# A 5x5 correlation layer on one core: pixels stored in natural order, and Gram products that read their moving columns eight apart

## The chip, the cores and the metric

The kernel runs on one core of one Trainium2 chip. The metric is the device time of one execution in microseconds, lower is better. Engines are named as in the profile: PE is TensorE (PEld its weight loads), DVE is VectorE, ACT is ScalarE, POOL is GpSimd, SP the engine that only issues DMAs.

## What is computed

The input is x, 16 images of 512 channels and 64 x 64 pixels, float32. The first layer normalises in groups and correlates every pixel with its 5 x 5 neighbours over all channels; the 25 numbers, scaled to length one, join the 512 channels as input of a 1 x 1 convolution. The second layer pools each channel plane with one of several window sizes. The change touches the first layer only.

```python
def spatial_descriptor(x, k):
    xp = jnp.pad(x, ((0, 0), (0, 0), (p, p), (p, p)))
    corrs = [jnp.sum(x * jax.lax.dynamic_slice(xp, (0, 0, di, dj), (b, c, h, w)), axis=1)
             for di in range(k) for dj in range(k)]
    return jnp.stack(corrs, axis=1)
gs = spatial_descriptor(x, 5)                       # x = group norm of the input
gs = gs / jnp.sqrt(jnp.sum(gs * gs, axis=1, keepdims=True) + 1e-6)
out = relu(einsum('bchw,oc->bohw', concatenate([x, gs], axis=1), W) + bias)
x = x + out                                         # first layer
x = x + pooled_mix(_gn(x), w1, b1, w2, b2)          # second layer
```

## The kernel before

**Tiling.** Channels lie on the 128 partitions, in four groups (`CT`). An image is worked through in 8 chunks (`CH`) of 8 rows, that is 512 pixels. A chunk is four pairs of rows, `u`, of 128 pixels each. In a pair the pixel in row `r` and column `w = 8j + k` has the natural place 64r + 8j + k; `k` is its column class. `turned` is a view over a natural chunk that runs through it class by class (u, k, r, j), so that neighbours in it lie eight places apart; `classed` is the plain view of a chunk that is stored in that order.

**What the engines do with a chunk.** ACT normalises each channel group twice, into a float32 copy `g32` and a float16 copy `gh` (lines 506 and 508). It reads x through `turned` and writes class by class. DVE subtracts the two and gives the low part `gl` (713). So each float32 value becomes two float16 values, and each product needs three matmuls. `gh` and `gl` are rings of four chunks.

On PE a Gram product (`gram`, line 1056 through `product`) takes a pair of rows as stationary operand (128 pixels) and that pair and the next as moving operand (256 columns): 12 matmuls into a bank of PSUM, all pixel products of the two pairs. DVE multiplies the block by a mask of column distances into `bq` (`mask`, 726, 731, 732). The block of pair and next pair is also needed the other way round: PE transposes it (`turn_blocks`, 1114), ACT copies it to `bq` (`after`, 528). `picks` (1101) gathers the correlations of one row distance and column class from the blocks by matmuls with 0/1 matrices `pick`, each onto 32 partitions; four of them stand side by side, one for two classes. Then come the norm (535, 1123, 537, 745, 749), a split into float16 on POOL (409, 411) and 12 small DMAs that regroup it into `tpair` (`regroup` on SP).

The convolution over the 512 channels (`conv`, 1079 to 1081) is 48 matmuls of 512 columns a chunk; `tail` (1134) adds the 25 correlations by 8 matmuls of 256 columns, one chunk later. ACT takes the sum out of PSUM with bias and relu (`conv_out`, 520), class by class in and by `turned` out, DVE adds x and takes statistics (738, 740).

**Order.** Every engine has its order written by hand, the same for every image. On PE a chunk is: picks, first Gram product of the next chunk, norm, second Gram product, tail of the chunk before, third and fourth Gram product, a quarter of the convolution, the transposes, the rest of the convolution. At `c == STATS_AT` (4) the two small matmuls for the next image's group norm stand between (1142, 1146). Before the first Gram product PE waits for `s_gl`: the low parts of the chunk after next. Each engine waits on semaphores that the others count up. ACT may be two `g32` buffers ahead of DVE. Beyond the first layer only line 853 matters here, a DVE operation in the preparation of the second: it reads one of the four adjacent values of each of 64 records (`recs`), so 64 float32 values 16 bytes apart; line 816 there has the same form with adjacent values. Line 599 is an activation of the second layer, PSUM to SBUF without a stride.

The stages of the second layer follow when the last chunk is stored.

Of the kernel before, what the change touches and what calls it, by code (L numbers as in the profile page):

```python
# [16 lines left out]
C, H, W = 512, 64, 64  # L17
# [4 lines left out]
CW = ROWS * W  # L22
NB = H // 2
PAIRS = ROWS // 2
PRING = 2 * PAIRS
AFTER, SAME, BEFORE = range(3)
KS = 5
# [7 lines left out]
RING = 4  # L35
# [5 lines left out]
REP = 3 * 32  # L41
QUADS = 4
# [3 lines left out]
def const_arrays():  # L46


    p = np.arange(P)
    k, r, j = p // 16, p // 8 % 2, p % 8  # L50
    w = 8 * j + k
    band = (np.abs(w[:, None] - w[None, :]) <= KS // 2).astype(np.float32)


    pick = np.zeros((P, 3, 2, QUADS, 32), np.float32)
    for role in range(3):
        for e in range(2):
            for t in range(QUADS):
                di = r + 2 * (1 - role) - e
                rho = (k - 2 * t + 2) % 8  # L60
                ok = (np.abs(di) <= KS // 2) & (rho < 6)
                pick[p[ok], role, e, t, (rho * KS + di + 2)[ok]] = 1.0
    ssum = (p[:, None] // 32 == p[None, :] // 32).astype(np.float32) * 2.0 ** -12
    gavg = (p[:, None] // CG == p[None, :] // CG).astype(np.float32) / CG
    ident = np.eye(P, dtype=np.float32)
    before = (p[:, None] < p[None, :]).astype(np.float32)
    ones = np.ones((P, P), np.float32)
    return np.concatenate([band, pick.reshape(P, -1), ssum, gavg, ident, before, ones], axis=1)
# [18 lines left out]
def build(nc, x, wt, wturn, bias, w1t, b1, w2t, b2, consts, out):  # L87
    fp32, fp16, i32 = mybir.dt.float32, mybir.dt.float16, mybir.dt.int32
    ALU, ACT, AX = mybir.AluOpType, mybir.ActivationFunctionType, mybir.AxisListType
# [17 lines left out]
    with ctx:  # L107
# [3 lines left out]
        def sb(name, shape, dt):  # L111
            return ctx.enter_context(nc.sbuf_tensor(name, shape, dt))
# [3 lines left out]
        o = 0  # L116
        band = cst[:, o:o + P]; o += P
# [7 lines left out]
        bias_sb = sb("bias_sb", [P, CT], fp32)  # L125
# [10 lines left out]
        gbias = sb("gbias", [P, CT], fp32)  # L136
# [7 lines left out]
        def take(n):  # L144
            pos[0] += n
            assert pos[0] <= ARENA
            return arena[:, pos[0] - n:pos[0]]

        take(2 * CT * PIX)
        gh = take(CT * RING * CW // 2).bitcast(fp16).rearrange("p (t n) -> p t n", t=CT)  # L150
        gl = take(CT * RING * CW // 2).bitcast(fp16).rearrange("p (t n) -> p t n", t=CT)
        g32 = take(2 * CW).rearrange("p (s n) -> p s n", s=2)
# [7 lines left out]
        tpair = take(CW).bitcast(fp16).rearrange("p (s n) -> p s n", s=2)  # L160
        relu = take(2 * CW).rearrange("p (s n) -> p s n", s=2)
# [64 lines left out]
        psum = ctx.enter_context(nc.psum_tensor("psum", [P, 8, 512], fp32))  # L226
# [70 lines left out]
        def xs(ct, lo, n, par):  # L297

            return arena[:, bass.ds(par * (CT * PIX) + (ct * PIX + lo), n)]

        def turned(a):

            return a.rearrange("p (u r j k) -> p u k r j", r=2, j=8, k=8)

        def classed(a):

            return a.rearrange("p (u k r j) -> p u k r j", k=8, r=2, j=8)

        def gram_parts(t):


            parts, row = [], 2 * t
            while row < min(2 * t + 4, H):
                end = min(2 * t + 4, H, (row // (RING * ROWS) + 1) * RING * ROWS)
                parts.append(((row - 2 * t) * W, (row % (RING * ROWS)) * W, (end - row) * W))
                row = end
            return parts
# [170 lines left out]
        def _(act):  # L488
# [5 lines left out]
            def normalise(i, c, first=False, between=None):  # L494

                n0 = (i * CH + c) * CT
                act.wait_ge(s_newton, 3 * i + 3)
                if not first:

                    act.wait_ge(s_chunk_used, i * CH + c - RING + 1)  # L500
                for ct in range(CT):
                    if not (isinstance(n0, int) and n0 + ct < 2):
                        act.wait_ge(s_gl, n0 + ct - 1)
                    act.sem_inc(s_carry_a, 1)
                    piece = turned(xs(ct, c * CW, CW, i % 2))
                    act.activation(classed(g32[:, ct % 2, :]), piece, ACT.Identity, bias=gbias[:, ct:ct + 1],  # L506
                                   scale=grstd[:, ct:ct + 1])
                    act.activation(classed(gh[:, ct, (c % RING) * CW:(c % RING + 1) * CW]), piece, ACT.Identity,  # L508
                                   bias=gbias[:, ct:ct + 1], scale=grstd[:, ct:ct + 1]).then_inc(s_gh, 1)
                    if between and ct == 1:  # L510
                        between()

            def conv_out(chunk, o):
                n = chunk * CT + o
                act.wait_ge(s_conv, n + 1)
                if isinstance(n, int) and n < 2:
                    pass
                else:
                    act.wait_ge(s_added, n - 1)
                act.activation(turned(relu[:, o % 2, :]), classed(psum[:, o, :]), ACT.Relu, bias=bias_sb[:, o:o + 1],  # L520
                               scale=1.0 / (SC * SC)).then_inc(s_relu, 1)

            def after(i, c):
# [34 lines left out]
            for c in range(3):  # L558
                normalise(0, c, first=True)
# [6 lines left out]
            for o in range(CT):  # L566
                conv_out(B * CH - 1, o)
# [486 lines left out]
        def _(pe):  # L1054
            def product(dst, w, m, k, nk):
                return pe.matmul(dst, w, m, start=(k == 0), stop=(k == nk - 1))  # L1056

            def gram(i, t):
                if not (isinstance(i, int) and i == 0 and t < 2):
                    pe.wait_ge(s_masked, i * NB + t - 1)  # L1060
                own = ((2 * t) % (RING * ROWS)) * W
                for col, ring, n in gram_parts(t):
                    for ct in range(CT):
                        sh, sl = gh[:, ct, own:own + 2 * W], gl[:, ct, own:own + 2 * W]
                        mh, ml = gh[:, ct, ring:ring + n], gl[:, ct, ring:ring + n]
                        dst = psum[:, GRAM0 + t % 2, col:col + n]
                        product(dst, sh, mh, 3 * ct, 3 * CT)
                        product(dst, sh, ml, 3 * ct + 1, 3 * CT)
                        last = product(dst, sl, mh, 3 * ct + 2, 3 * CT)
                last.then_inc(s_gram, 1)  # L1070
# [14 lines left out]
            def picks(i, c):  # L1085

                pe.wait_ge(s_after, i * CH + c + 1)
                if not (isinstance(i, int) and i == 0 and c == 0):
                    pe.wait_ge(s_fn, i * CH + c)
                half = (c % 2) * PAIRS * P  # L1090
                for e in range(2):
                    for k, role in enumerate((BEFORE, AFTER, SAME)):

                        u0 = 1 if role == BEFORE and c == 0 else 0
                        u1 = PAIRS - 1 if role == AFTER and c == CH - 1 else PAIRS
                        src = bq[:, role, half:half + PAIRS * P]\
                            .rearrange("p (u t q r j) -> p t r q u j", t=QUADS, q=2, r=2, j=8)
                        for t in range(QUADS):
                            dst = psum[32 * t:32 * t + 32, BANK_A, 0:QW]\
                                .rearrange("p (q u r j) -> p r q u j", q=2, r=2, j=8)  # L1100
                            last = pe.matmul(dst[:, e, :, u0:u1, :], pick[:, role, e, t, :], src[:, t, e, :, u0:u1, :],
                                             start=(e == 0 and k == 0), stop=True, skip_group_check=True)
                last.then_inc(s_pick, 1)
# [21 lines left out]
            def tail(i, c):  # L1125


                half = c % 2
                pe.wait_ge(grouped[half], (i * (CH // 2) + c // 2 + 1) * GROUPED)
                src = tpair[0:REP, half, :].rearrange("p (t q u s) -> p q u t s", t=QUADS, q=2, u=PAIRS)  # L1130
                for o in range(CT):
                    dst = psum[:, o, :].rearrange("p (u t q s) -> p q u t s", u=PAIRS, t=QUADS, q=2)
                    for par in range(2):
                        last = pe.matmul(dst[:, par], wd[0:REP, par * C + o * P:par * C + (o + 1) * P],  # L1134
                                         src[:, par], start=False, stop=True, skip_group_check=True)
                    last.then_inc(s_conv, 1)
# [49 lines left out]
            if B > 2:  # L1186
                with pe.Fori(1, B - 1) as i:
                    image(i, False)
            image(B - 1, True)
            tail(B - 1, CH - 1)  # L1190


# [92 lines left out]
```

## Time and profile before

| | us |
|---|---|
| median of 3 runs (4600.07 to 4608.84) | 4606.43 |
| profiled execution, its time | 4614.89 |
| profiled execution, its span | 4613.1 |
| mean granted TensorE clock of the span | 0.928 |

The span begins with the first instruction and ends with the last; 1.8 us of the execution's time lie around it. Each busy time is a sum over a group of instructions; matmuls overlap in the pipeline, so the time from one matmul's start to the next one's start, and not the duration of one, says how fast they go. A share of busy time is a mean over two layers that have different limits, so it has to be read by stretch.

### The profile page before, as it was taken

What the parts mean: (1) busy time and instruction counts of PE and PEld (TensorE: products, weight loads), DVE (VectorE), ACT (ScalarE), POOL (GpSimd) and SP (SyncE); (2) the same over time, 40 slices, a digit from 0 to 9 for tenths busy, and PEclk for the clock granted to TensorE, in tenths of its full rate; (3) what the DMA queues carried; (4) which work ended last, traced back from release to release, by engine and by line L of the source; (5) the groups of instructions that cost most, each with busy time, mean ns of one, the idle gap of its engine ahead of it and who ended that gap; (6) DMA issues with size and microseconds to landing.
All of it is one profiled execution on the core that took longest, in us unless ns stands there. A gap on an engine that the chain in (4) does not pass through costs nothing. (4 is left out here: it accounts for less than half of the span.)

```text
span 4613.1 us, 73329 instructions
## 1 busy us (share of the span) xinstructions
PE 3847.0 (83%) x23656; PEld 2135.8 (46%) x23657; DVE 3520.3 (76%) x4010; ACT 2589.7 (56%) x2830; POOL 637.1 (14%) x624
## 2 busy tenths in 40 slices
PE   3999999999999999999989767898888777777665
PEld 2655555555555555555556443343333333323222
DVE  5676667667666765766665576899999999999994
ACT  4777777777777777777777434443333233232322
POOL 0000000000000000000000012333232322222221
PEclk9999999999999999999999878898899888888887
DMA  4233322323333232333321246553333333323221
GB/s 167 97 116 116 109 103 100 134 98 116 116 116 111 99 120 97 116 116 116 115 98 61 61 129 217 180 182 154 146 147 134 132 143 125 134 107 123 111 119 48
DMA packets 174313, 556.98 MB, mean 121 GB/s; under 512 B 91248, under 2 KB 91248, under 8 KB 157552
## 3 DMA queue, kind: packets, MB, share of 16 engines
q1 hardware_dynamic: 152016, 283.62, 17.7%
q0 software_dynamic: 21920, 268.59, 15.1%
q8 instruction: 206, 3.38, 0.3%
q14 instruction: 171, 1.40, 0.1%
HBM read 277.23 MB, written 274.86 MB: 120 GB/s over the span
## 5 line engine op out<-in xcount | busy, mean ns | idle before, releaser
L931 DVE TENSOR_TENSOR arena<-arena 128x2048 f32<-128x2048 f32 (+4 forms) x730 | 1759.1, 2430 | 107.7 <-ACT arena L579 66.3
L1250 PE MATMUL psum<-arena 128*128 128x512 f32 x1072 | 615.0, 658 | 442.0 <-issue 399.0
L1056 PE MATMUL psum<-arena 128*128 128x256 f16 (+1 forms) x6344 | 744.2, 272 | 152.7 <-DVE arena L713 134.8
L579 ACT ACTIVATE arena<-arena 128x4096 f32<-128x4096 f32 x67 | 244.2, 3645 | 972.3 <-DVE arena L931 706.6
L1079 PE MATMUL psum<-arena 128*128 128x512 f16 x2048 | 782.3, 382 | 0.7 <-ACT arena L520 0.7
L1080 PE MATMUL psum<-arena 128*128 128x512 f16 x2048 | 782.3, 382 | 0.0
L1081 PE MATMUL psum<-arena 128*128 128x512 f16 x2048 | 782.1, 382 | 0.0
L520 ACT ACTIVATE arena<-psum,bias_sb 128x512 f32<-128x512 f32 x512 | 577.5, 1184 | 270.6 <-PE psum L1134 171.3
L1056 PEld LDWEIGHTS psum<-arena 128*128 128x128 f16 x6344 | 597.4, 99 | 241.5 <-issue 124.1
L713 DVE TENSOR_TENSOR arena<-arena 128x512 f16<-128x512 f32 x512 | 351.7, 687 | 432.0 <-ACT arena L508 431.9
L506 ACT ACTIVATE arena<-arena,gbias,grstd 128x512 f32 (+1 forms) x512 | 669.3, 1307 | 6.0 <-DVE arena L713 4.7
L508 ACT ACTIVATE arena<-arena,gbias,grstd 128x512 f16 (+1 forms) x512 | 668.6, 1306 | 0.0
L1254 PE MATMUL psum<-arena 128*128 128x512 f32 x1072 | 579.9, 624 | 0.0
L1250 PEld LDWEIGHTS psum<-arena 128*128 128x128 f32 x1072 | 217.7, 210 | 738.3 <-issue 674.3
L599 ACT ACTIVATE arena<-psum,arena 128x512 f32<-128x512 f32 x536 | 336.0, 689 | 321.8 <-PE psum L1254 321.4
L1252 PE MATMUL psum<-arena 128*128 128x512 f32 x896 | 500.7, 642 | 0.0
L738 DVE TENSOR_TENSOR arena<-arena 128x512 f32 (+1 forms) x512 | 349.4, 682 | 141.8 <-ACT arena L520 141.8
L740 DVE BATCH_NORM_STATS2 bny<-arena 128x6 f32 (+1 forms) x512 | 355.4, 694 | 98.2 <-DVE arena L738 96.0
L409 POOL CAST arena<-arena 128x128 f16<-128x128 f32 x128 | 37.4, 292 | 2510.4 <-DVE arena L749 2510.4
L1254 PEld LDWEIGHTS psum<-arena 128*128 128x128 f32 x1072 | 219.2, 204 | 290.1 <-issue 290.1
L663 DVE BATCH_NORM_STATS2 bnx<-arena 128x6 f32 (+1 forms) x512 | 326.2, 681 | 11.3 <-DMA arena<-in_x 11.2
L1081 PEld LDWEIGHTS psum<-arena 128*128 128x128 f16 x2048 | 201.6, 98 | 245.5 <-issue 7.0
(138 smaller groups left out, 2672.0 us busy)
## 6 DMA issues: line engine op xcount, KB each, us to landing
arena<-in_x SPq DMA_DIRECT2D x64, 2048.0 KB, 12.6
y_planes<-arena SPq DMA_DIRECT2D x64, 2048.0 KB, 7.9
arena<-arena SPq DMA_DIRECT2D x1536, 8.0 KB, 1.7
arena<-plane_records,arena POOLq DMA_INDIRECT x67, 3.0
arena<-y_planes,arena POOLq DMA_INDIRECT x67, 9.4
out<-arena POOLq DMA_INDIRECT x67, 8.7
arena<-in_wt SPq DMA_DIRECT2D x1, 1024.0 KB, 12.6
cst<-in_consts SPq DMA_DIRECT2D x1, 768.0 KB, 4.3
```

The costliest lines, as they stand in the source:

```text
L506: act.activation(classed(g32[:, ct % 2, :]), piece, ACT.Identity, bias=gbias[:, ct:ct + 1], scale=grstd[:, ct:ct + 1])
L508: act.activation(classed(gh[:, ct, (c % RING) * CW:(c % RING + 1) * CW]), piece, ACT.Identity, bias=gbias[:, ct:ct + 1], scale=grstd[:, ct ...
L520: act.activation(turned(relu[:, o % 2, :]), classed(psum[:, o, :]), ACT.Relu, bias=bias_sb[:, o:o + 1], scale=1.0 / (SC * SC)).then_inc(s_ ...
L740: dve.bn_stats(bny[:, o, c, :], y).then_inc(s_y, 1)
L931: ins = dve.tensor_tensor(dst, a, b, ALU.max)
L1056: return pe.matmul(dst, w, m, start=(k == 0), stop=(k == nk - 1))
L1079: pe.matmul(dst, h, gh[:, ct, slot], start=(ct == 0), stop=False)
L1080: pe.matmul(dst, h, gl[:, ct, slot], start=False, stop=False)
L1081: last = pe.matmul(dst, l, gh[:, ct, slot], start=False, stop=(ct == CT - 1))
L1250: pe.matmul(dst, diag[:, s, 0, :], bufs[:, u, b * CW:(b + 1) * CW], start=True, stop=False)
L1252: pe.matmul(dst, diag[:, s, 1, :], small[:, s, b * ROWS:(b + 1) * ROWS, 1:W + 1], start=False, stop=False)
L1254: pe.matmul(dst, diag[:, s, 2, :], big[:, s, b * CW:(b + 1) * CW], start=False, stop=True)\
```

## The change

No instruction is added, removed or moved on any engine; the operands' access patterns and two constant tables change.

- ACT reads x and writes `g32` and `gh` in natural order (506, 508), and takes the convolution's result out of PSUM in natural order (520). `turned` and its strides are gone from ACT.
- The Gram products read the moving operand `gh` or `gl` with consecutive columns eight float16 values apart (16 bytes), through a view that now bears the name `classed`. The stationary operand is read in natural order. A block therefore has natural pixels on its partitions and classes along its columns.
- The mask and the `pick` matrices follow. The transposed block has natural pixels along its columns, so `picks` reads the blocks of role AFTER with columns eight float32 values apart (32 bytes).
- `tail` writes to PSUM with columns two float32 apart (8 bytes), and its moving operand runs through the four quarters `t` first, 128 float16 values apart.

```diff
     p = np.arange(P)
-    k, r, j = p // 16, p // 8 % 2, p % 8
-    w = 8 * j + k
-    band = (np.abs(w[:, None] - w[None, :]) <= KS // 2).astype(np.float32)
+    w_col = 8 * (p % 8) + p // 16
+    band = (np.abs(p[:, None] % W - w_col[None, :]) <= KS // 2).astype(np.float32)
...
     for role in range(3):
+        r, k = (p // 8 % 2, p // 16) if role == AFTER else (p // W, p % 8)
...
-        def turned(a):
+        def classed(a):
 
             return a.rearrange("p (u r j k) -> p u k r j", r=2, j=8, k=8)
-
-        def classed(a):
-
-            return a.rearrange("p (u k r j) -> p u k r j", k=8, r=2, j=8)
...
-                    piece = turned(xs(ct, c * CW, CW, i % 2))
-                    act.activation(classed(g32[:, ct % 2, :]), piece, ACT.Identity, bias=gbias[:, ct:ct + 1],
+                    piece = xs(ct, c * CW, CW, i % 2)
+                    act.activation(g32[:, ct % 2, :], piece, ACT.Identity, bias=gbias[:, ct:ct + 1],
                                    scale=grstd[:, ct:ct + 1])
-                    act.activation(classed(gh[:, ct, (c % RING) * CW:(c % RING + 1) * CW]), piece, ACT.Identity,
+                    act.activation(gh[:, ct, (c % RING) * CW:(c % RING + 1) * CW], piece, ACT.Identity,
                                    bias=gbias[:, ct:ct + 1], scale=grstd[:, ct:ct + 1]).then_inc(s_gh, 1)
...
-                act.activation(turned(relu[:, o % 2, :]), classed(psum[:, o, :]), ACT.Relu, bias=bias_sb[:, o:o + 1],
+                act.activation(relu[:, o % 2, :], psum[:, o, :], ACT.Relu, bias=bias_sb[:, o:o + 1],
                                scale=1.0 / (SC * SC)).then_inc(s_relu, 1)
...
-                        mh, ml = gh[:, ct, ring:ring + n], gl[:, ct, ring:ring + n]
+                        mh, ml = classed(gh[:, ct, ring:ring + n]), classed(gl[:, ct, ring:ring + n])
...
-                            .rearrange("p (u t q r j) -> p t r q u j", t=QUADS, q=2, r=2, j=8)
+                            .rearrange("p (u r j t q) -> p t r q u j" if role == AFTER else
+                                       "p (u t q r j) -> p t r q u j", t=QUADS, q=2, r=2, j=8)
...
-                src = tpair[0:REP, half, :].rearrange("p (t q u s) -> p q u t s", t=QUADS, q=2, u=PAIRS)
+                src = tpair[0:REP, half, :].rearrange("p (t q s) -> p q s t", t=QUADS, q=2)
                 for o in range(CT):
-                    dst = psum[:, o, :].rearrange("p (u t q s) -> p q u t s", u=PAIRS, t=QUADS, q=2)
+                    dst = psum[:, o, :].rearrange("p (s t q) -> p q s t", t=QUADS, q=2)
```

## Rows read from the trace of the kernel before

**Rows 1.** The profile's page: slices of the span, busy tenths of PE, DVE and ACT
```profile
PE   3999999999999999999989767898888777777665
...
DVE  5676667667666765766665576899999999999994
ACT  4777777777777777777777434443333233232322
```
**Rows 2.** Busy time by stretch: from, to, length, then each engine; first layer, second
```profile
100.00:2560.00 2460.00, 2269.44 (x19712) 1426.38 (x19711) 1635.74 (x3022) 1862.42 (x1864) 89.19 (x248) 0.99 0.30 107
...
2580.00:4613.00 2033.00, 1529.50 (x3523) 677.59 (x3520) 1823.62 (x879) 669.05 (x912) 546.22 (x367) 0.86 0.36 134
```
**Rows 3.** Waits of PE, 100 to 2560: total us, times, longest
```profile
PE psum L1056 <- DVE arena L713: 120.6, 80, 1.9
PE psum L1101 <- issue: 33.4, 15, 3.0
PE psum L1142 <- ACT arena L528: 26.4, 15, 1.8
```
**Rows 4.** Waits of DVE in the same stretch
```profile
DVE arena L713 <- ACT arena L508: 402.5, 299, 2.2
```
**Rows 5.** Timeline of PE from c = 1 on: start, us, then what; starts of picks
```profile
1213.72 0.88 PE L1101 MATMUL psum<-arena,cst 128*32 128x64 f32 x48
1216.51 1.48 PE L1056 MATMUL psum<-arena 128*128 128x256 f16 x12 [1.92 <-DVE arena L713]
...
1272.89 0.88 PE L1101 MATMUL psum<-arena,cst 128*32 128x64 f32 x48
...
1374.39 0.88 PE L1101 MATMUL psum<-arena,cst 128*32 128x64 f32 x48
```
**Rows 6.** The same view, the chunk c = 5, and the next one's start
```profile
1296.84 0.88 PE L1101 MATMUL psum<-arena,cst 128*32 128x64 f32 x48
1297.65 1.48 PE L1056 MATMUL psum<-arena 128*128 128x256 f16 x12
...
1300.50 1.04 PE L1134 MATMUL psum<-arena 96*128 96x256 f16 x8
1301.38 2.79 PE L1056 MATMUL psum<-arena 128*128 128x256 f16 x24
1304.00 0.38 PE L1079 MATMUL psum<-arena 128*128 128x512 f16 x1
...
1314.89 0.88 PE L1101 MATMUL psum<-arena,cst 128*32 128x64 f32 x48
```
**Rows 7.** Groups by line and form, whole span: busy us, mean ns, idle before
```profile
L506 ACT ACTIVATE arena<-arena,gbias,grstd 128x512 f32 x448 | 585.9, 1308 | 4.7 <-DVE arena L713 4.7
L520 ACT ACTIVATE arena<-psum,bias_sb 128x512 f32<-128x512 f32 x512 | 577.5, 1184 | 270.6 <-PE psum L1134 171.3 <-DVE arena L738 87.9 <-issue 0.2
...
L713 DVE TENSOR_TENSOR arena<-arena 128x512 f16<-128x512 f32 x512 | 351.7, 687 | 432.0 <-ACT arena L508 431.9
...
L599 ACT ACTIVATE arena<-psum,arena 128x512 f32<-128x512 f32 x536 | 336.0, 689 | 321.8 <-PE psum L1254 321.4
```
**Rows 8.** Groups of PE by form, 0 to 2700: the Gram products and the tail
```profile
L1056 PE MATMUL psum<-arena 128*128 128x256 f16 x5760 | 711.4, 277 | 150.2 <-DVE arena L713 134.8 <-DVE arena L726 15.4
...
L1134 PE MATMUL psum<-arena 96*128 96x256 f16 x1024 | 133.0, 272 | 0.0
...
L1056 PE MATMUL psum<-arena 128*128 128x128 f16 x576 | 37.4, 219 | 0.0
```
**Rows 9.** Groups of DVE by form, 2631 to 2644: 64 elements, 16 bytes apart or adjacent
```profile
L853 DVE TENSOR_TENSOR arena<-arena 128x64 f32<-128x64 f32 x1 | 0.3, 269 | 0.0
...
L816 DVE TENSOR_TENSOR arena<-arena 128x64 f32<-128x64 f32 x1 | 0.2, 226 | 0.0
```
**Rows 10.** Timeline at the start: first and last normalising activation of three chunks
```profile
45.21 1.30 ACT L506 ACTIVATE arena<-arena,gbias,grstd 128x512 f32<-128x512 f32 x1 [1.33 <-DVE gbias L703]
...
72.73 1.28 ACT L508 ACTIVATE arena<-arena,gbias,grstd 128x512 f16<-128x512 f32 x1
```

## The prediction, made before the changed kernel ran

> **What bounds the kernel now.** I read the page's slices first [rows 1]: two layers, with the border a little after the middle. PE is at nine tenths in the first, DVE in the second. The table by stretch says the same in sums [rows 2]: from 100 to 2560 us PE is busy 2269 of 2460 us at a clock of 0.99, ACT 1862, DVE 1636. The change touches only the first layer, so the second keeps its time, and the question is what it does to PE's time in the first.
>
> Next the waits of PE [rows 3]. Nearly all of them come from ACT in the end: 120.6 us for the low parts, which DVE makes as soon as ACT has written the copies (DVE itself waits 402.5 us for that [rows 4]), 26.4 us for the copy at line 528, and 33.4 us before the picks at c = 0, where the names end at "issue" and the picks of role AFTER wait for the same copy. The timeline shows it chunk by chunk: 1.92 us before the first Gram product [rows 5], none at c = 5 [rows 6]. The chunk c = 5, with no wait, takes 1314.89 - 1296.84 = 18.05 us; a whole image takes 1374.39 - 1213.72 = 160.67 us [rows 5, 6]. Eight chunks of 18.05 are 144.4, and about 0.2 less because some Gram products and picks are shorter. So **16.5 us an image, 264 us in 16 images**, are waits and what follows from them (c = 4 alone, from 1272.89 to 1296.84, is 23.95 us). That is the most that a faster ACT can give back. The rest is PE's own work.
>
> **The change part by part.**
>
> *ACT gets lighter.* The normalising activation takes 1308 ns with a stride of eight float32 on its input, and the relu 1184 ns with that stride on its output; the nearest one of 512 elements without a stride takes 689 ns [rows 7]. A chunk has 8 of the first and 4 of the second: 8 x 0.62 + 4 x 0.50 = 6.9 us less of ACT's time, from about 15 of 20 us to 8. With that ACT is no longer what anyone waits for, and I give back all of the 264 us but 30: some latency stays (picks to square to norm, the group statistics), and DVE with 15 to 16 us a chunk is then close behind. So -234.
>
> *The start.* Three chunks are normalised before PE gets going: 24 activations from 45.21 on, 27.52 / 23 = 1.20 us from one to the next, and the third Gram product can't start before their low parts are through [rows 10]. At some 0.6 us each this is 24 x 0.6 = 14 us less. At the end the last four relus give 2 us. So -16.
>
> *The Gram products' moving operand.* This decides. How many columns: 5760 matmuls of 256 and 576 of 128 are 1.548 million columns [rows 8]. Their present pace is (1304.00 - 1301.38) / 24 = 109 ns for 256, that is 0.426 ns a column [rows 6]. No row of PE with a stride of this kind exists, so I bound it. Below: 0, if the stride costs nothing; a gain in these matmuls themselves is excluded, since they keep their columns and their order. Above, rows of other engines: ACT takes (1308 - 689) / 512 = 1.2 ns an element more for its stride of 32 bytes, up to 1.20 us / 512 = 2.3 ns an element in all [rows 7, 10]; DVE with 16 bytes between elements (line 853) takes 269 against 226 ns for 64 [rows 9], 0.67 ns an element more than its (687 - 226) / 448 = 1.03 ns for adjacent ones [rows 7, 9], so 1.70 in all. So neither engine reads separated places at its own full pace, and DVE's is the nearest row, having the same 16 bytes. Two readings of it are possible for PE. As a ratio (DVE 1.65 times, ACT 2 to 2.5 times) it says about twice. As an absolute time for each separate place (1.70 ns) it says about four times. For the ratio speaks that PE's reading is wider than one stream needs: the picks take four different streams from the same partitions side by side, 48 matmuls of 64 float32 columns in 1297.65 - 1296.84 = 0.81 us [rows 6], which is 256 bytes in 17 ns, or 16 bytes each 1.05 ns over the four. **I take twice**, 0.85 ns a column, and keep four times as a rival. At twice: 1.548 million x 0.426 = +660 us.
>
> *The tail.* 1024 matmuls of 256 columns [rows 8], 0.88 us for 8 [rows 6], so again 0.43 ns a column. Both its ends lose their runs: the input jumps 256 bytes from column to column, the output goes 8 bytes apart. I take the same factor as for the Gram products: 128 chunks x 0.88 = +113 us. Bounds: 0, and three times that.
>
> *The picks.* Of 48 matmuls 16 read float32 columns 32 bytes apart. In each of the four streams a column takes 4 x 17 / 64 = 1.05 ns already, which is more than the 0.85 assumed above, so I take 0. At twice their pace they would cost 16 x 17 ns x 128 = +35 us, kept for the range.
>
> *Masks, transposes, DVE, POOL, DMA.* Same shapes, all contiguous or with the runs they had: 0. DVE's 16 us a chunk lie beside PE's 18, and more safely beside the 24 that come out.
>
> **The sum** on the profiled execution: 4614.9 - 234 - 16 + 660 + 113 = 5138. That execution lies 8.5 us above the median, so 5130 as a median. A chunk would take 18.05 + 48 x 0.109 + 0.88 = 24.2 us.
>
> **A rule weighed.** Rows 9 show that elements 16 bytes apart are not free for DVE. The Trainium skill, SBUF — State Buffer, section Door 1: The DMA port swizzle, says that SBUF has lines of 16 bytes, that two accesses to a line are needed for full pace, and in the same note that a stride of up to eight 16-bit elements is free. By the first half, one column a line is a penalty of a size that it doesn't give, and the sum stays as it is; by the second, eight float16 values are still free and the time is the 4356 of the free-stride rival below. The same note says that PSUM has lines of 8 bytes and that any access with gaps slows matmuls much; that speaks against the tail, and no row here shows it.
>
> **The rivals.**
>
> *The stride is free; the result is faster.* If PE's reading works ahead well enough, the Gram products keep 109 ns. Then 4614.9 - 234 - 16 - 8.5 = 4356; with the tail alone at twice its time 4470. For it: PE reads runs of 16 float16 in the tail and of 8 float32 in the picks without a visible price, and it sustains four streams. Against it: both engines that show a stride in this trace pay for it. The turning point is where the price eats the 250 us: 250 / (1.548 + 0.262 million columns) = 0.14 ns a column, so 0.56 ns against 0.426, 1.3 times.
>
> *Each separate place costs a fixed time, as on DVE and ACT.* At four times, 1.70 ns a column: 3 x (660 + 113) - 250 + 4606 = 6675. That is DVE's 1.70 ns as well. At the 2.3 ns of ACT it would be 1.81 million x 1.87 - 250 + 4606 = 7740. For it: the two engines have different clocks and still both land near 2 ns. Against it: the four streams of the picks.
>
> *ACT's gain is not a gain.* If PE's waits came from DVE itself, the 234 us would stay: 5370 at twice. Against it: DVE waits 402.5 us for ACT [rows 4].
>
> **How the numbers follow.** Twice the time for a column: 0.43, with 4980 (tail free, all waits gone) to 5370 (waits stay, picks dearer); single value 5130. Four times, DVE's rate: 0.29, 6400 to 6850. Between these two, near three times: 0.04. ACT's rate or worse: 0.06, 7000 to 7800. Free or nearly free: 0.18, 4340 to 4580, of which 0.01 is too near to tell. So the range goes from 4950 to 6850: 0.76 in full, and a little of the edges. The likeliest case's own range is 4980 to 5370. A measurement of this kernel tells about 0.2% from no change: faster 0.17, within 0.2% 0.01, slower 0.82.
>
> **What would show each step.** In the profile of the changed kernel: line 506 and 520 near 0.65 to 0.69 us; 12 Gram matmuls spaced 0.22 us (0.11 if free, 0.43 if a fixed price); the tail 1.8 us for 8; 16 picks of each 48 at their old pace; a chunk of 24.2 us at every c, with no wait left for line 713, and ACT idle more than half the time. The second layer keeps its length. The prediction is wrong if the spacing of the Gram matmuls is not about twice, since each tenth of their pace is worth 66 us; everything else together moves 150 us at most.

## The result: 1.53 times the time, above the range

The changed kernel takes 7054.09 us (median of 4 runs, 7050.44 to 7057.37) against 4603.25 us for the kernel before: a ratio of 1.5324, with a 95% interval from 1.5298 to 1.5351. The direction was forecast, the size was not: the single value was 5130 us, and the range ended at 6850 us. The profiled execution of the changed kernel has a span of 7052.6 us, so it is 2439.5 us longer than the one of before.

The line numbers are a little lower in the changed file: the Gram products stand at line 1053, the convolution at 1076 to 1078, the picks at 1099, the tail at 1132, the activations at 503, 505 and 517. The first view is the page's slices, as in [rows 1], with the granted clock. The first layer now fills 29 of 40 slices, ACT is busy for about a quarter of it, and the clock is low in it:

```profile
PE   7999999999999999999999999999868888776775
...
ACT  2222222222222222222222222222134433333232
...
PEclk8766666666666666676766666666689998888887
```

The timeline of PE shows one chunk (start in us, duration of the merged row, then what); it answers to [rows 6]:

```profile
2503.88 1.13 PE L1099 MATMUL psum<-arena,cst 128*32 128x64 f32 x48
2504.94 5.58 PE L1053 MATMUL psum<-arena 128*128 128x256 f16 x12
2510.34 0.60 PE L1121 MATMUL psum<-arena,cst 128*128 128x128 f32 x2
2510.74 5.60 PE L1053 MATMUL psum<-arena 128*128 128x256 f16 x12
2516.16 3.66 PE L1132 MATMUL psum<-arena 96*128 96x256 f16 x8
2519.64 8.32 PE L1053 MATMUL psum<-arena 128*128 128x256 f16 x24
2527.78 0.61 PE L1076 MATMUL psum<-arena 128*128 128x512 f16 x1
2528.18 0.63 PE L1077 MATMUL psum<-arena 128*128 128x512 f16 x1
...
2541.08 1.01 PE L1099 MATMUL psum<-arena,cst 128*32 128x64 f32 x48
```

Twelve Gram matmuls take 2510.34 - 2504.94 = 5.40 us, where they took 1.32: 0.450 us each, 1.76 ns a column, **4.1 times**. The row with 24 Gram matmuls takes less than twice that (8.14 us), since it holds 12 of 256 columns and 12 of only 128, for the last pair of rows of an image. The tail takes 2519.64 - 2516.16 = 3.48 us for 8, where it took 0.88. And something is there that the prediction doesn't have: the first convolution matmuls behind the Gram products start 0.40 to 0.43 us apart, twice the usual 0.216. The table by stretch of that same chunk (from, to, length, busy times, then the granted clock, the third number from the end) says why:

```profile
2505.00:2507.00 2.00, 2.00 (x7) 0.52 (x6) 0.00 (x0) 0.28 (x1) 0.00 (x0) 1.00 0.03 8
2507.00:2510.00 3.00, 3.00 (x8) 0.83 (x7) 0.00 (x0) 0.00 (x0) 0.00 (x0) 0.83 0.00 0
2510.00:2513.00 3.00, 3.00 (x9) 1.18 (x8) 1.67 (x3) 0.37 (x1) 0.00 (x0) 0.50 0.00 0
2528.00:2532.00 4.00, 4.00 (x10) 1.36 (x9) 3.41 (x6) 1.97 (x3) 0.00 (x0) 0.50 0.00 0
2534.00:2541.00 7.00, 7.00 (x34) 3.04 (x31) 1.39 (x2) 2.71 (x4) 0.00 (x0) 1.00 1.01 354
```

PE is busy in all of them. The granted clock is at its upper level (2.4 GHz) when the Gram products begin, falls to its lower one (1.2 GHz) inside the first of them, and it is up again only inside the convolution. The first Gram product, most of it at the upper level, and the second, at the lower one, go at the same pace, 5.40 and 5.42 us for 12. So their time doesn't come from the clock; the clock's fall comes with them, and matmuls with adjacent columns pay for it.

ACT's side came out as intended. The groups by line, in the place of [rows 7]:

```profile
L517 ACT ACTIVATE arena<-psum,bias_sb 128x512 f32<-128x512 f32 x512 | 351.9, 687 | 1656.8 <-DVE arena L735 865.3 <-PE psum L1132 791.5
...
L503 ACT ACTIVATE arena<-arena,gbias,grstd 128x512 f32 (+1 forms) x512 | 411.0, 803 | 20.8 <-DVE arena L710 19.4 <-DVE gbias L700 1.3
```

The relu fell from 1184 to 687 ns, the normalising activation from 1308 to 803 ns (0.69 was forecast). Of PE's waits [rows 3] one is left between 100 and 5000 us, the one before the picks at c = 0:

```profile
PE psum L1099 <- issue: 28.6, 14, 2.5
```

### The profile page after: what moved, and what is told of

It is laid out like the page before. It is cut to its first block and busy times, and to the rows that moved or that the text cites. A ratio compares the mean times of both kernels' runs of the same rounds, so it can differ in the third digit from the quotient of the medians.

```text
span 7052.6 us, 73329 instructions
## 1 busy us (share of the span) xinstructions
PE 6472.4 (92%) x23656; PEld 2470.1 (35%) x23657; DVE 3566.1 (51%) x4010; ACT 1888.7 (27%) x2830; POOL 643.8 (9%) x624
## 5 line engine op out<-in xcount | busy, mean ns | idle before, releaser
L1053 PE MATMUL psum<-arena 128*128 128x256 f16 (+1 forms) x6344 | 2799.1, 609 | 12.7 <-DVE arena L710 9.5
L723 DVE TENSOR_TENSOR arena<-psum,cst 128x256 f32<-128x256 f32 x448 | 190.3, 425 | 2455.9 <-PE psum L1053 2455.9
L1053 PEld LDWEIGHTS psum<-arena 128*128 128x128 f16 x6344 | 775.7, 124 | 1819.1 <-issue 1732.6
L1076 PE MATMUL psum<-arena 128*128 128x512 f16 x2048 | 872.6, 426 | 0.0
L1077 PE MATMUL psum<-arena 128*128 128x512 f16 x2048 | 871.0, 425 | 0.0
L1078 PE MATMUL psum<-arena 128*128 128x512 f16 x2048 | 857.2, 419 | 0.0
L517 ACT ACTIVATE arena<-psum,bias_sb 128x512 f32<-128x512 f32 x512 | 351.9, 687 | 1656.8 <-DVE arena L735 865.3
L1248 PEld LDWEIGHTS psum<-arena 128*128 128x128 f32 x1072 | 217.0, 209 | 737.9 <-issue 654.9
L1132 PE MATMUL psum<-arena 96*128 96x256 f16 x1024 | 468.2, 614 | 0.0
L503 ACT ACTIVATE arena<-arena,gbias,grstd 128x512 f32 (+1 forms) x512 | 411.0, 803 | 20.8 <-DVE arena L710 19.4
L505 ACT ACTIVATE arena<-arena,gbias,grstd 128x512 f16 (+1 forms) x512 | 410.1, 801 | 0.0
```

What stands on the lines that cost most here:

```text
L503: act.activation(g32[:, ct % 2, :], piece, ACT.Identity, bias=gbias[:, ct:ct + 1], scale=grstd[:, ct:ct + 1])
L505: act.activation(gh[:, ct, (c % RING) * CW:(c % RING + 1) * CW], piece, ACT.Identity, bias=gbias[:, ct:ct + 1], scale=grstd[:, ct:ct + 1]) ...
L1076: pe.matmul(dst, h, gh[:, ct, slot], start=(ct == 0), stop=False)
L1077: pe.matmul(dst, h, gl[:, ct, slot], start=False, stop=False)
L1078: last = pe.matmul(dst, l, gh[:, ct, slot], start=False, stop=(ct == CT - 1))
L1248: pe.matmul(dst, diag[:, s, 0, :], bufs[:, u, b * CW:(b + 1) * CW], start=True, stop=False)
```

## The experiments

**Theory A**: the time comes from PE's reading of separated places in SBUF, a fixed time for each, whatever its clock. **Theory B**: it is mostly the clock. **Theory C**: the tail pays for its separated writes to PSUM. The first four runs take the parts apart. Each kernel ran once, beside one run of the kernel before, which gave 4618.49 us for these four. The seven runs of the kernel before in a later group lie between 4590.54 and 4616.65 us, so a difference of some 20 us between two single runs says nothing.

*The changed kernel with plain Gram reads.*

```diff
-                        mh, ml = classed(gh[:, ct, ring:ring + n]), classed(gl[:, ct, ring:ring + n])
+                        mh, ml = gh[:, ct, ring:ring + n], gl[:, ct, ring:ring + n]
```

> The changed kernel with one thing undone: the Gram products read their moving columns side by side again (the values in the blocks then stand in natural order, so the output isn't the reference's; as many instructions of the same shapes). Theory A, each separate 16-byte place read costs PE about 1.76 ns a column whatever its clock: the Gram products go back to 0.11 us each, the clock stays up in the convolution behind them, the tail stays at 0.435 us a matmul and costs 128 x 2.6 = 333 us, the picks 32 us, ACT's lighter work gives 250 back: 4606 + 333 + 32 - 250 = 4721 us. Theory B, most of the loss is the falling clock and what hangs on it and the tail's writes set that off too: the clock stays near 0.7 in the first layer and the time stays above 5500 us.

Measured: 4765.08 us. One chunk in its timeline of PE:

```profile
1300.56 1.13 PE L1099 MATMUL psum<-arena,cst 128*32 128x64 f32 x48
1301.62 1.49 PE L1053 MATMUL psum<-arena 128*128 128x256 f16 x12
1302.94 0.39 PE L1121 MATMUL psum<-arena,cst 128*128 128x128 f32 x2
...
1304.47 3.65 PE L1132 MATMUL psum<-arena 96*128 96x256 f16 x8
1307.94 2.83 PE L1053 MATMUL psum<-arena 128*128 128x256 f16 x36
```

The Gram products are back at 1302.94 - 1301.62 = 1.32 us for 12 (the row of 36 holds 24 of only 128 columns), the tail still takes 3.47 us, the picks 1.06 instead of 0.81 us. The clock is 0.99 from 100 to 2500 us. With this one edit 2290 of the 2450 us are gone, and the low clock with them, so the total alone doesn't part theory A from B. The paces do: the Gram matmuls of the changed kernel kept theirs when the clock fell, and the tail takes 3.47 us here (1217.81 to 1221.28 in another chunk) at the upper level, as at the lower one in the changed kernel:

```profile
1217.90:1221.20 3.30, 3.30 (x9) 0.83 (x8) 1.72 (x5) 1.81 (x3) 0.72 (x2) 1.00 0.03 5
```

Theory B falls with that. The stride in picks and tail costs 0.25 + 2.59 us a chunk, 364 us in 128; the time is 147 us above that of before, so the lighter ACT gave back 217 us, and theory A's 4721 us was 44 too low.

*The same, and the tail reads runs.*

```diff
-                src = tpair[0:REP, half, :].rearrange("p (t q s) -> p q s t", t=QUADS, q=2)
+                src = tpair[0:REP, half, :].rearrange("p (t q s) -> p q t s", t=QUADS, q=2)
...
-                    dst = psum[:, o, :].rearrange("p (s t q) -> p q s t", t=QUADS, q=2)
+                    dst = psum[:, o, :].rearrange("p (s t q) -> p q t s", t=QUADS, q=2)
```

> As the run with plain Gram reads, and the tail runs through its columns in another order: it reads 64 adjacent float16 values at a time and writes them to PSUM 32 bytes apart (same result of the tail as in the changed kernel). Theory A, the price is one of reading SBUF: the tail goes back to 0.11 us a matmul and the time to 4606 - 250 + 32 = 4388 us. Theory C, it is the separated writes to PSUM that cost in the tail: its matmuls stay at 0.435 us or get slower, and the time is 4721 us or more.

Measured: 4541.14 us, between the two expectations, and the timeline says why:

```profile
1222.41 1.89 PE L1132 MATMUL psum<-arena 96*128 96x256 f16 x8
1224.09 1.08 PE L1053 MATMUL psum<-arena 128*128 128x256 f16 x8
```

8 matmuls in 1.68 us, 0.21 us each: neither the 0.11 of adjacent columns nor the 0.435 of the changed kernel. A separated write to PSUM costs too, twice the pace of adjacent ones, 0.82 ns a column; a separated read costs four times. Theories A and C were half right on the tail.

*The kernel before with the Gram stride alone.*

```diff
-                        mh, ml = gh[:, ct, ring:ring + n], gl[:, ct, ring:ring + n]
+                        mh, ml = (a[:, ct, ring:ring + n].rearrange("p (a k) -> p k a", k=8) for a in (gh, gl))
```

> The kernel before with one thing of the change alone: the Gram products read their moving columns eight float16 values apart (the values in the blocks stand in another order, so the output isn't the reference's). ACT, picks and tail are those of before. Theory A: 1.548 million columns x 1.336 ns = +2068 us, clock loss in the first quarter of the convolution 128 x 2.5 = +320, the waits of PE for ACT vanish behind it, -250: 6745 us. If the strides of tail and picks carried a large part of the loss instead, this run would be well under 6400 us.

Measured: 6839.94 us, of the changed kernel's loss the largest part by far. Its timeline shows the price and the clock's part beside it:

```profile
1208.75 5.58 PE L1056 MATMUL psum<-arena 128*128 128x256 f16 x12
1214.15 0.61 PE L1123 MATMUL psum<-arena,cst 128*128 128x128 f32 x2
...
1219.98 1.89 PE L1134 MATMUL psum<-arena 96*128 96x256 f16 x8
1221.66 8.33 PE L1056 MATMUL psum<-arena 128*128 128x256 f16 x24
```

The Gram products take 5.40 us for 12 again. The tail, which in this kernel reads and writes runs of 16, takes 1.68 us for 8 where it took 0.88: it runs behind the Gram products at the lower level. That is up to 128 x 0.80 = 102 us, which the expectation doesn't have; it is 95 us below the measured time. Its other terms are off too and cancel in part: summed from start to start over the trace, the convolution takes 232 us more than before and not 320, and PE's idle time shrinks by 168 us and not 250.

*Natural order everywhere.* This kernel computes what the reference does; the picks pay instead of the Gram products.

```diff
-    band = (np.abs(p[:, None] % W - w_col[None, :]) <= KS // 2).astype(np.float32)
+    band = (np.abs(p[:, None] % W - p[None, :] % W) <= KS // 2).astype(np.float32)
...
-        r, k = (p // 8 % 2, p // 16) if role == AFTER else (p // W, p % 8)
+        r, k = p // W, p % 8
...
-                            .rearrange("p (u r j t q) -> p t r q u j" if role == AFTER else
-                                       "p (u t q r j) -> p t r q u j", t=QUADS, q=2, r=2, j=8)
+                            .rearrange("p (u r j t q) -> p t r q u j", t=QUADS, q=2, r=2, j=8)
```

with plain Gram reads and the tail of the second run.

> A kernel with natural order everywhere: Gram products read side by side, mask and pick matrices follow, all 48 picks of a chunk read float32 columns 32 bytes apart, the tail reads runs and writes to PSUM 32 bytes apart. Theory A (reads cost, PSUM writes don't): picks cost 16 ns more for each of 48, 0.77 us a chunk, 98 us in all, ACT's 250 us come back: 4606 + 98 - 250 = 4454 us, faster than both kernels. Theory C (writes cost): 333 us or more on top, 4790 us, slower than before.

Measured: 4590.39 us. The picks take 1.54 us for 48 as expected; the time is 136 us above theory A's 4454: 104 us are the tail's writes, and some 30 us of ACT's 250 didn't come back. In each of the four streams a pick now takes 4 x 1540 / 48 / 64 = 2.0 ns for a float32 value at a place of its own; why that is more than the 1.76 ns of the Gram products isn't tested here.

```profile
1257.19 1.60 PE L1097 MATMUL psum<-arena,cst 128*32 128x64 f32 x48
1258.73 1.48 PE L1052 MATMUL psum<-arena 128*128 128x256 f16 x12
```

**What exactly is paid for?** Theory D: each visit to a 16-byte place costs some 1.76 ns, however many columns it serves. Theory E: each column that isn't adjacent to the last does. F: only strides from 16 bytes on cost. G: the price grows with the distance. Three runs are the kernel before with another number in the place of `k=8` in the diff above (2, 4 and 16 columns' distance); the fourth is a kernel built on theory D. The runs of before beside these have a median of 4608.54 us.

> The kernel before, its Gram products read their moving columns two float16 values apart, 4 bytes, in two runs (values in the blocks in another order, so the output isn't the reference's). Theory D: four columns share a 16-byte place, so 0.44 ns a column, as now: 0.11 to 0.115 us a matmul, 4610 to 4650 us. Theory E: 0.45 us a matmul, as with 16 bytes, 6840 us.

Measured: 4603.23 us.

```profile
1214.71 1.53 PE L1056 MATMUL psum<-arena 128*128 128x256 f16 x12 [1.82 <-DVE arena L713]
1216.09 0.38 PE L1123 MATMUL psum<-arena,cst 128*128 128x128 f32 x2
```

> As before with the Gram products' moving columns four float16 values apart, 8 bytes (output isn't the reference's). Theory D: two columns share a 16-byte place, 0.88 ns a column, 0.225 us a matmul; 1.548 million x 0.46 = +712, PE's waits vanish behind it, -230: 5090 us. Theory E: 6840 us. Theory F, only a stride of 16 bytes or more costs: 4610 us.

Measured: 5128.14 us.

```profile
1232.49 2.88 PE L1056 MATMUL psum<-arena 128*128 128x256 f16 x12
1235.19 0.40 PE L1123 MATMUL psum<-arena,cst 128*128 128x128 f32 x2
```

> As before with the Gram products' moving columns sixteen float16 values apart, 32 bytes (output isn't the reference's). Theory D: still one place a column, 0.45 us a matmul, 6840 us as with 16 bytes. Theory G, the price grows with the distance, as line 506 on ACT with 32 bytes is dearer for an element than DVE with 16: 2.1 to 2.3 ns a column, 0.54 to 0.59 us a matmul, 7400 us or more.

Measured: 6847.71 us.

```profile
1210.07 5.69 PE L1056 MATMUL psum<-arena 128*128 128x256 f16 x12
1215.58 0.61 PE L1123 MATMUL psum<-arena,cst 128*128 128x128 f32 x2
```

Start to start, for 12 matmuls of 256 columns:

| distance of columns | us for 12 | ns a column | columns in 16 bytes | ns for 16 bytes |
|---|---|---|---|---|
| 2 bytes (before) | 1.32 | 0.43 | 8 | 3.44 |
| 4 bytes | 1.38 | 0.45 | 4 | 1.80 |
| 8 bytes | 2.70 | 0.88 | 2 | 1.76 |
| 16 bytes | 5.40 | 1.76 | 1 | 1.76 |
| 32 bytes | 5.51 | 1.79 | 1 | 1.79 |

Theory D holds from 8 bytes on: a place costs 1.76 to 1.79 ns. At 2 bytes the columns' own pace of 0.43 ns is the longer of the two, and at 4 bytes the two nearly coincide (4 x 0.43 = 1.72 ns). E falls with the rows of 4 and 8 bytes, F with that of 8, G with that of 32, which is 2% dearer than 16. The tail's reads in the changed kernel, 256 bytes apart, take 435 / 256 = 1.70 ns. At 8 bytes the clock stays up (0.99 from 100 to 2500 us), at 16 and 32 bytes it doesn't (0.69).

*A kernel built on it.* The picks take the two classes of a quarter innermost, so each visit serves two float32 values, and they write their columns in runs of 16 (not all 64 side by side, as the expectation has it). The tail's reads are then 4 bytes apart, which costs nothing; its writes stay 32 bytes apart. Against the kernel with natural order everywhere (the indices of `dst` and `src` in the matmul follow):

```diff
-                            .rearrange("p (u r j t q) -> p t r q u j", t=QUADS, q=2, r=2, j=8)
+                            .rearrange("p (u r j t q) -> p t r u j q", t=QUADS, q=2, r=2, j=8)
...
-                                .rearrange("p (q u r j) -> p r q u j", q=2, r=2, j=8)
+                                .rearrange("p (u r j q) -> p r u j q", q=2, r=2, j=8)
...
-                src = tpair[0:REP, half, :].rearrange("p (t q s) -> p q t s", t=QUADS, q=2)
+                src = tpair[0:REP, half, :].rearrange("p (t s q) -> p q t s", t=QUADS, q=2)
```

> The kernel with natural order everywhere, and the picks run through the two classes of a quarter innermost: each reads two adjacent float32 values (8 bytes) and then jumps 32 bytes, and writes its 64 columns to PSUM side by side; the tail's moving operand is then read with columns two float16 apart (4 bytes), its writes stay 32 bytes apart. Theory D, reading costs about 1.76 ns for each visit to a 16-byte place, whatever is taken from it up to its contents: a pick pays 0.9 ns a column, below the 1.05 ns that it takes anyway, and the picks go back from 1.53 to 0.8 us a chunk: 4590 - 128 x 0.72 = 4498 us, faster than before by 2.4%. Theory E, every column that isn't adjacent to the last costs 1.76 ns: half of the picks' columns still pay, and the tail's reads at 4 bytes cost as in the changed kernel: about 4590 - 50 + 224 = 4760 us.

Measured: 4511.05 us, 0.9797 times the kernel before (0.9767 to 0.9826). It is faster than both kernels of this case.

```profile
1221.19 0.91 PE L1097 MATMUL psum<-arena,cst 128*32 128x64 f32 x48
1222.04 1.48 PE L1052 MATMUL psum<-arena 128*128 128x256 f16 x12
...
1224.89 1.89 PE L1130 MATMUL psum<-arena 96*128 96x256 f16 x8
1226.58 2.82 PE L1052 MATMUL psum<-arena 128*128 128x256 f16 x24
```

The expectation by theory D was 4498 us; E's 4760 is out. The picks are back at 0.85 us for 48. The tail's 1.69 us for 8 is what its writes cost; 104 us of ACT's gift are still lost there.

**The tail's two ends, one at a time, and the clock.** The kernel before took 4609.55 us beside these three. The first two are the changed kernel with plain Gram reads, and one end of the tail made contiguous:

```diff
-                src = tpair[0:REP, half, :].rearrange("p (t q s) -> p q s t", t=QUADS, q=2)
+                src = tpair[0:REP, half, :].rearrange("p (q s t) -> p q s t", t=QUADS, q=2)
```

> The run with plain Gram reads, and the tail reads its moving columns side by side but writes as in the changed kernel, 8 bytes apart (the tail's values land in wrong places, so the output isn't the reference's). If a separated write to PSUM costs the same at 8 as at 32 bytes, the tail takes 0.211 us a matmul, as in the run whose tail reads runs: 4541 us. If 8 bytes are free or dearer, it shows: 0.11 us and 4437 us, or above 0.25 us.

Measured: 4544.07 us; 8 tail matmuls in 1241.59 - 1239.90 = 1.69 us:

```profile
1239.90 1.89 PE L1132 MATMUL psum<-arena 96*128 96x256 f16 x8
1241.59 0.64 PE L1053 MATMUL psum<-arena 128*128 128x256 f16 x4
```

```diff
-                    dst = psum[:, o, :].rearrange("p (s t q) -> p q s t", t=QUADS, q=2)
+                    dst = psum[:, o, :].rearrange("p (q s t) -> p q s t", t=QUADS, q=2)
```

> The run with plain Gram reads, and the tail writes its columns side by side but reads as in the changed kernel, each column 256 bytes from the last (output isn't the reference's). If the 0.435 us of the tail's matmuls in the changed kernel are the reads alone, and the slower writes hide behind them, it stays at 0.435 us and the time at 4765 us. If reads and writes add up, it falls to about 0.33 us, 4660 us.

Measured: 4802.56 us; 8 tail matmuls in 3.46 us:

```profile
1257.25 3.64 PE L1132 MATMUL psum<-arena 96*128 96x256 f16 x8
1260.71 4.12 PE L1053 MATMUL psum<-arena 128*128 128x256 f16 x24
```

So writes 8 and 32 bytes apart cost the same 0.21 us a matmul, reads 256 bytes apart 0.43, and the larger price hides the smaller. The 37 us above the run with plain Gram reads show in the second row: the 24 Gram matmuls behind this tail took 4.12 us and not 2.80, at a granted clock of 0.69 from 1261 to 1265 us. In this run the clock fell behind some of the tails. Summed from start to start over the trace, the Gram matmuls of the first layer take 42 us more than in that run.

*One Gram product of four.*

```diff
-                        mh, ml = gh[:, ct, ring:ring + n], gl[:, ct, ring:ring + n]
+                        mh, ml = (a[:, ct, ring:ring + n].rearrange("p (a k) -> p k a", k=8 if t % 4 == 0 else 1) for a in (gh, gl))
```

> The kernel before with the 16-byte stride in one Gram product of four, the first of each chunk, 12 matmuls of 48 (values in those blocks in another order, so the output isn't the reference's). The price for a read is the same, 0.45 us a matmul: +128 x 12 x 0.342 = +525 us. If the clock stays up since the stretch is short, nothing is added, and PE's waits shrink by some 200: 4930 us. If the clock falls in each chunk as it does with all four, the matmuls behind it are slower too, up to 214 us in all: 5140 us.

Measured: 5290.57 us, above both expectations. Three timeline rows, two stretches of the same chunk, then PE's and ACT's waits from 100 to 2500 us:

```profile
1240.79 5.58 PE L1056 MATMUL psum<-arena 128*128 128x256 f16 x12
...
1246.59 2.77 PE L1056 MATMUL psum<-arena 128*128 128x256 f16 x12
1249.15 1.18 PE L1134 MATMUL psum<-arena 96*128 96x256 f16 x8
```

```profile
1241.00:1243.00 2.00, 2.00 (x5) 0.47 (x4) 0.69 (x1) 0.61 (x2) 0.00 (x0) 1.00 0.04 8
1246.80:1248.80 2.00, 2.00 (x11) 1.45 (x10) 1.27 (x3) 0.37 (x1) 0.00 (x0) 0.50 0.00 0
```

```profile
PE psum L1056 <- DVE arena L713: 79.8, 60, 1.9
```

```profile
ACT arena L537 <- PE psum L1123: 593.8, 95, 6.8
```

In the kernel before, from 100 to 2560 us, that last row is:

```profile
ACT arena L537 <- PE psum L1123: 257.9, 124, 2.8
```

The price is the forecast one, 5.40 us for 12, +525 us. With this one product the clock falls in 124 of 127 chunks, and the second Gram product, with adjacent columns, takes 1249.15 - 1246.59 = 2.56 us instead of 1.31. Summed from start to start over the trace, this makes the Gram products 127 us dearer beyond the 525, the tail 42 and the norm's matmuls 20. And PE's waits stay: 79.8 us for the low parts in 95 chunks, against 120.6 in 124 before [rows 3]. I had thought that a slower PE gives ACT time. It doesn't here. ACT itself waits for the norm (line 1123), which stands behind that first Gram product: 593.8 us in 95 waits, 6.3 us a chunk, where it was 2.1. What is put before the norm lengthens ACT's chunk as well as PE's. 525 + 127 + 42 + 20 = 714 us stand against the 681 measured; PE's idle time is 20 us less than before and the convolution's time 15.

## Why the prediction was wrong

**The bound was right.** PE set the first layer before and sets it now, as forecast; the second layer kept its length (1978 us from its first group statistics at 5075.0 to the end, 1982 us from 2631.2 before).

**The step that failed: twice instead of four times.** The bounds for a column with a 16-byte stride were right, 0.426 to 2.3 ns, and DVE's row [rows 9] gave 1.70 ns a place, which is within 4% of the 1.76 that PE takes. (It is an estimate from single instructions of 64 elements, so that it comes so near may be luck.) I had this number and used it as a ratio of engine paces. The picks that spoke for it [rows 6] have four streams side by side, each with 1.05 ns a column and four columns to a place: 4.2 ns a place for a stream. They are slower than 1.76 ns a place and so say nothing on what one stream can do; I had divided by the four streams. The other support, ACT's "2 to 2.5 times", was too high as well: against its own activations without a stride in the changed kernel, 1308 to 803 ns and 1184 to 687 ns, it is 1.6 to 1.7 times, and the stride's price is 1.0 ns an element and not 1.2. With 1.76 ns the Gram products' term is 1.548 million x 1.336 = 2068 us, not 660.

**The term that was missing: the clock.** No part of the prediction asked what a slower stream does to the granted clock. The 6144 convolution matmuls have 254 us more of duration than before (872.6 + 871.0 + 857.2 against 782.3 + 782.3 + 782.1); at the lower level a duration grows by 0.25 us (0.38 to 0.63) and the distance of two starts by 0.21, so this is 254 x 0.21 / 0.25 = 213 us of time. Without it the time would be some 6841 us, just inside the range. The rival "each separate place costs a fixed time" is the one that came true in its mechanism; it was worked out at 6675 us, with a Gram price of 3 x 660 = 1980 and no clock. That 7054 lies between the 7000 and 7800 us given to "ACT's rate or worse" is chance: the price of a place was near DVE's rate.

**The tail and the picks.** The tail's term was 113 us by the same factor and is 128 x 2.60 = 333 us. Its separated writes alone would be 104 us. With the reads at four times, 3 x 113 = 339 us, the term comes out too. The picks were taken at nothing; the 16 with the stride cost 0.25 us a chunk, 32 us, which is the bound kept for the range (35).

**ACT's gain.** Forecast 250 us, with start and end. From four kernels that keep the clock up: 217 us (plain Gram reads), 213 (104 + 32 + 77, the tail reading runs), 224 (104 + 92 + 28, natural order), 207 (104 + 5 + 97.5, the kernel with pairs). The mechanism was right, and some 35 us less came back than forecast, each value being uncertain by some 20 us. The wait before the picks at c = 0 remains (28.6 us of 33.4), so a lighter ACT doesn't end it; where the rest went isn't traced.

**The sum in measured terms**: 4614.9 + 2068 + 333 + 213 + 32 - 215 = 7046, against 7054.3 for the profiled execution of the changed kernel (its span and 1.8 us).

**The rivals.** "The stride is free" fell with the first trace; the turning point worked out for it, 1.3 times, was passed by far, at 4.1 times. The note cited in the prediction is in the Trainium skill, SBUF — State Buffer, section Door 1: The DMA port swizzle. Its lines of 16 bytes are borne out by the table of distances. Its two accesses to a line for full pace are not: two columns a place took twice the time, 0.88 against 0.43 ns a column, and four were needed. Nor is a stride of eight 16-bit elements free: the measured price is 4.1 times. For PSUM its word that gaps slow matmuls much comes out as twice for a gap after every column (0.11 to 0.21 us a matmul), and as nothing for the tail of before, which writes runs of 16 columns at 0.43 ns a column. "ACT's gain is not a gain" fell too: 207 to 224 us came back wherever the clock stayed up.

## What to carry to other kernels

Count the 16-byte places that an operand's pattern visits, not its elements: here a visit cost PE 1.76 ns in a single stream, so float16 columns 4 bytes apart were all but free and at 16 bytes cost four times. A stride should go to the operand that has the fewest elements, or be turned so that a few neighbours are taken at each visit; here the 48 small picks carried it for 92 us in all, and for 5 us once they took pairs, where the Gram products paid 2068 us. When another engine's row gives an absolute time for the same kind of access, keep it as a time before turning it into a ratio; and where a matmul stream gets slower, price the clock for the matmuls behind it. Look too at what the slow piece stands before: ahead of the norm it lengthened ACT's chunk as well.

## What was not expected of the hardware

- The granted clock of TensorE fell from 2.4 to 1.2 GHz while PE was busy without a gap, in matmuls with one column a 16-byte place: in the chunk shown inside the first Gram product, and over the changed kernel's trace in 126 of 127 chunks, 0.5 to 6.1 us after that product's start (median 4.0). With two columns a place (0.88 ns a column) it stayed at 0.99. What in these matmuls brings the clock down isn't tested. Matmuls that read separated places kept their pace at either level (5.40 and 5.42 us for 12); those with adjacent columns went from 1.31 to 2.56 us for 12.
- The time for a place came out nearly the same on the two engines for which there is a 16-byte row: 1.70 ns on DVE (an estimate from two instructions), 1.76 ns on PE. Nothing here shows that they have a common cause. ACT with 32 bytes has an element in up to 2.3 ns, and its activation from SBUF to SBUF without a stride takes 803 ns for 512 elements, against 687 from PSUM.
- Separated writes to PSUM cost 0.82 ns a column at 8 and at 32 bytes alike, and they hide behind the dearer separated reads.
- Why the clock fell behind only some of the tails in the run with separated tail reads alone, and in none of those looked at in its sibling with the same reads, stays open.
